# Building the stacked rank-16 factors on chip from eight raw copies, with VectorE and GpSimd in place of SBUF-to-SBUF transfers

## The reference, cut to what matters

```python
z1 = einsum('bfi,bir->bfr', x, u) / 512
z  = einsum('bfr,bor->bfo', z1, u) / 16
y  = einsum('bfi,oi->bfo', x, W) + fc_bias + z + cond
out = x + gelu(y)            # exact gelu, all in fp32
```

## Time and profile before

| | us |
|---|---|
| median of 3 runs | 387.24 (386.15 to 387.47) |
| the profiled execution's own time | 387.57 |
| its span, first to last instruction | 385.8 |
| TensorE busy | 376.9 (98% of the span) |
| VectorE busy | 296.7 (77%) |
| ScalarE busy | 204.6 (53%) |
| GpSimd busy | 0.7 |
| mean granted TensorE clock | 0.995 of full speed |
| DMA queue of SyncE | 27088 packets, 84.41 MB, 71.8% of the 16 engines' span |

### The profile page before, as it was taken

The page is one execution under the profiler, slowest core; times in us unless marked ns, Lnnn a source line. Parts: engine busy times, 40 slices in busy tenths (PEclk is TensorE's granted clock), DMA queues, the critical chain, the costliest instruction groups (busy, mean ns, idle before and its releaser), DMA issues.

```text
span 385.8 us, 7835 instructions
## 1 busy us (share of the span) xinstructions
PE 376.9 (98%) x3065; PEld 313.8 (81%) x3065; DVE 296.7 (77%) x188; ACT 204.6 (53%) x214; POOL 0.7 (0%) x5
## 2 busy tenths in 40 slices
PE   8998899999999999999999999999999999999995
PEld 3676788888888888888888888888888888888884
DVE  2579967788877878888777897778888787788832
ACT  3467364545566445566545556654465664455531
POOL 0000000000000000000000000000000000000000
PEclk9999899999999999999999999999999999999999
DMA  7879789887777877777787777687767779774222
GB/s 193 229 152 304 220 268 270 265 263 233 213 231 225 261 221 248 211 218 234 239 244 231 244 212 221 213 266 220 256 230 206 230 218 270 216 255 131 110 109 110
DMA packets 27756, 85.75 MB, mean 222 GB/s; under 512 B 6832, under 2 KB 6960, under 8 KB 23776
## 3 DMA queue, kind: packets, MB, share of 16 engines
q1 hardware_dynamic: 27088, 84.41, 71.8%
q10 hardware_dynamic: 656, 1.18, 1.0%
HBM read 35.75 MB, written 33.55 MB: 180 GB/s over the span
## 4 chain that ended last, share of the span: by engine, by line
PE 89%; SPq 5%; DMA 2%; ACTq 1%; ACT 1%; DVE 1%; issue 0%
PE y L420 82%; SPq L178 5%; PE update L489 3%; DMA f_stack<-f_parts 2%; ACTq L274 1%; PE y L404 1%; PE y L412 1%; PE y L408 1%; ACT L279 0%; SPq L164 0%; SPq L192 0%; ACT result L270 0%; DVE result L356 0%; DVE x_low L313 0%; DVE f_parts L313 0%
## 5 line engine op out<-in xcount | busy, mean ns | idle before, releaser
L420 PE MATMUL y<-x_low,w_high 64*128 64x512 f32 x928 | 184.5, 388 | 0.0
L420 PE MATMUL y<-x_high,w_high 64*128 64x512 f32 x928 | 184.5, 388 | 0.0
L270 ACT ACTIVATE result<-y,bias 128x512 f32<-128x512 f32 x128 | 81.4, 685 | 156.9 <-PE y L420 148.6
L420 PE MATMUL y<-x_high,w_low 64*128 64x512 f32 x928 | 125.2, 387 | 0.0
L356 DVE TENSOR_TENSOR result<-result,x_in 128x1024 f32<-128x1024 f32 (+1 forms) x65 | 78.3, 1205 | 56.5 <-ACT result L270 56.5
L420 PEld LDWEIGHTS y<-x_high,w_low 64*128 64x128 f32 x928 | 90.5, 185 | 15.3
L420 PEld LDWEIGHTS y<-x_low,w_high 64*128 64x128 f32 x928 | 90.5, 185 | 15.3
L420 PEld LDWEIGHTS y<-x_high,w_high 64*128 64x128 f32 x928 | 90.3, 185 | 15.3
L317 DVE SCALAR_TENSOR_TENSOR full_w<-update,base_w 128x2048 f32<-128x2048 f32 (+1 forms) x38 | 74.3, 1954 | 23.6 <-PE update L489 16.9
L313 DVE TENSOR_TENSOR x_low<-x_in,x_high 128x2048 fp32r<-128x2048 f32 (+1 forms) x38 | 74.0, 1947 | 5.6 <-ACT x_high L256 5.6
L313 DVE TENSOR_TENSOR w_low<-full_w,w_high 128x2048 fp32r<-128x2048 f32 (+1 forms) x38 | 74.0, 1948 | 0.4
(11 more groups left out here) (15 smaller groups left out, 29.7 us busy)
## 6 DMA issues: line engine op xcount, KB each, us to landing
out_t<-result SPq DMA_DIRECT2D x63, 512.0 KB, 3.1
x_in<-x_t SPq DMA_DIRECT2D x31, 1024.0 KB, 6.5
f_stack<-f_parts SPq DMA_DIRECT2D x186, 64.0 KB, 4.1
f_stack<-f_parts SPq DMA_DIRECT2D x124, 32.0 KB, 3.8
x_in<-x_t ACTq DMA_DIRECT2D x4, 256.0 KB, 9.3
base_w<-w_t SPq DMA_DIRECT2D x4, 256.0 KB, 8.2
f_parts<-factors SPq DMA_DIRECT2D x1, 896.0 KB, 6.8
out_t<-result SPq DMA_DIRECT2D x2, 256.0 KB, 2.5
```

What stands on the lines that cost most here:

```text
L270: nc.scalar.activation(result[j % SLOTS][:, m, :], y[m][:, :], ACT.Gelu, bias=bias[:, bass.ds(b * CHUNKS + m, 1)]).then_inc(gelu_ready, 1)
L420: return nc.tensor.matmul(y[m][:, :], w[rows, c, m * P:(m + 1) * P], x[rows, c, :], start=first, stop=last)
```

## The change

- The factors lie raw in DRAM, one [16, 512] matrix a batch. One DMA a batch reads it eight times over and fills the 128 rows of `f_raw` (four buffers). SyncE's 310 stack transfers are gone.
- Per batch ScalarE rounds all 128 rows (`high_factors`, L243), VectorE makes the weight side of the stack in one instruction, raw - high on the rows that are to hold the low part and raw elsewhere (`stack_factors`, L342), and GpSimd makes the moving side in two: `f_masked` = high * mask (L443) and raw + `f_masked` (L446). The mask is 0 or -1 for each row; GpSimd numbers the rows and VectorE turns the numbers into masks, once, at the start. The high blocks now hold the raw value, which TensorE takes in its place.
- TensorE's update waits for both sides. In the first two batches, the update of batch 1 stands ahead of piece 3 (before: ahead of piece 2) and waits for `full_w` chunk by chunk; the four first updates all stand ahead of piece 0, and `f_first` has 128 rows, of which 16 hold factors and the others zeros (two memsets on VectorE, the rest from DRAM).
- First loads: the weights lie chunk by chunk in DRAM; ScalarE's queue no longer loads factors between its first x chunks; SyncE issues the factors of batch 1 between the second and third weight chunk, and factors and x of batches 2 and 3 straight behind, with no wait.

Core of the diff:

```diff
-    STACK_DMAS = 5 * TILES
+    COPIES = P // RANK
...
         @block.sync
-            def stack_factors(t, j):
...
-                for copy in range(TILES):
...
-                        sp.dma_start(f_stack[slot][row + g * RANK:row + (g + 1) * RANK, sides, :].bitcast(fp32),
-                                     pair).then_inc(stacked[slot], 16)
-            sp.dma_start(f_first[:, :], factors[0:RANK, 0, :]).then_inc(f_first_loaded, 16)
+            def load_factors(t, j):
+                sp.dma_start(f_raw[j][:, :],
+                             factors[bass.ds(UNROLL * t + j, 1)].to_broadcast([COPIES, RANK, FEATURES])
+                             ).then_inc(f_loaded[j], 16)
+            sp.dma_start(f_first[0:FIRST_ROWS, :], first_factors).then_inc(f_first_loaded, 16)
             for c in range(CHUNKS):
-                sp.dma_start(base_w[:, c, :], w_t[:, c, :]).then_inc(w_loaded[c], 16)
+                sp.dma_start(base_w[:, c, :], w_t[c]).then_inc(w_loaded[c], 16)
+                if c == 1:
+                    load_factors(0, 1)
             load_x(0, 1)
...
-            sp.wait_ge(f_low_ready, 1)
-            stack_factors(0, 1)
-            stack_factors(0, 2)
-            sp.dma_start(f_parts[:, 1:GROUPS, 2, :], factors[:, 1:GROUPS, :]).then_inc(f_loaded[1], 16)
-            for j in range(2, X_SLOTS):
-                load_x(0, j)
+            load_factors(0, 2)
+            load_x(0, 2)
+            load_factors(0, 3)
+            load_x(0, 3)
...
         @block.scalar
+            def high_factors(t, j):
+                b = UNROLL * t + j
+                act.wait_ge(f_loaded[j], 16 * (t + 1) if j else 16 * t)
...
+                nc.scalar.activation(f_high[j % SLOTS][:, :], f_raw[j][:, :], ACT.Copy).then_inc(f_high_ready, 1)
...
                 elif not is_last(t, j):
                     split_x(tn, jn)
                     split_w(tn, jn)
+                    if not piecewise(t, j) and has_stack(t, j):
+                        high_factors(*stacked_in(t, j))
                 for m in range(CHUNKS if is_whole(t, j) else TILES):
                     gelu(t, j, m)
                 if piecewise(tn, jn):
                     for c in range(CHUNKS // 2, CHUNKS):
                         high_pieces(b + 1, c)
-                if j == 0 and not last_group:
-                    split_factors(t + 1)
+                if piecewise(t, j):
+                    high_factors(*stacked_in(t, j))
...
         @block.vector
+                nc.vector.scalar_tensor_tensor(f_stack[slot][:, 0, :], f_high[slot][:, :].bitcast(fp32),
+                                               low_rows[:, 0:1], f_raw[j][:, :], ALU.mult,
+                                               ALU.add).then_inc(weights_stacked, 1)
...
+            nc.vector.memset(f_first[FIRST_ROWS:2 * FIRST_ROWS, :], 0.0).then_inc(f_first_zeroed, 1)
+            nc.vector.memset(f_first[2 * FIRST_ROWS:P, :], 0.0).then_inc(f_first_zeroed, 1)
...
+                if has_stack(t, j):
+                    stack_factors(*stacked_in(t, j))
                 if piecewise(t, j):
                     finish_previous(t, j)
...
         @block.gpsimd
+                nc.gpsimd.tensor_scalar(f_masked[:, :], f_high[slot][:, :].bitcast(fp32), low_rows[:, 1:2], None,
+                                        ALU.mult).then_inc(factors_masked, 1)
+                pool.wait_ge(factors_masked, b)
+                nc.gpsimd.tensor_tensor(f_stack[slot][:, 1, :], f_raw[j][:, :], f_masked[:, :],
+                                        ALU.add).then_inc(moving_stacked, 1)
+            for b in range(1, BATCHES):
+                stack_factors(*divmod(b, UNROLL))
...
         @block.tensor
-            for c in range(CHUNKS - 1):
+            for c in range(CHUNKS):
                 first_update(c)
             for c in range(CHUNKS):
-                if c == 1:
-                    first_update(CHUNKS - 1)
-                if c == CHUNKS // 2:
+                if c == CHUNKS - 1:
                     rank_update(0, 1)
                 piece(0, c)
```

More of the change, by code:

```diff
@@ L39, in cond_residual_kernel @@
     GROUPS = BATCHES // UNROLL
-    RANK = factors.shape[0] // UNROLL
+    RANK = factors.shape[1]
+    FIRST_ROWS = first_factors.shape[0]
+    COPIES = P // RANK
     UPDATE_SCALE = 1.0 / (FEATURES * RANK)
@@ L72, in cond_residual_kernel @@
         result = [sb(f"result{s}", [P, CHUNKS, ROWS], fp32) for s in range(SLOTS)]
-        f_first = sb("f_first", [RANK, FEATURES], fp32)
-        f_parts = sb("f_parts", [UNROLL * RANK, GROUPS, 3, FEATURES], fp32)
+        f_first = sb("f_first", [P, FEATURES], fp32)
+        f_raw = [sb(f"f_raw{s}", [P, FEATURES], fp32) for s in range(UNROLL)]
+        f_high = [sb(f"f_high{s}", [P, FEATURES], fp32r) for s in range(SLOTS)]
+        f_masked = sb("f_masked", [P, FEATURES], fp32)
+        rows = sb("rows", [P, 1], int32)
+        row_bit = sb("row_bit", [P, 2], int32)
+        low_rows = sb("low_rows", [P, 2], fp32)
         f_stack = [sb(f"f_stack{s}", [P, 2, FEATURES], fp32r) for s in range(SLOTS)]
@@ L157, in previous_batch, with stacked_in, has_stack @@
             return (t, j - 1) if j else (t - 1, UNROLL - 1)
+        def stacked_in(t, j):
+            return t + (j + 2) // UNROLL, (j + 2) % UNROLL
+        def has_stack(t, j):
+            return not (isinstance(t, int) and t == GROUPS - 1 and j >= UNROLL - 2)
         block = ctx.enter_context(nc.Block())
@@ L199, in step @@
                 last_group = isinstance(t, int) and t == GROUPS - 1
-                if not (last_group and j >= UNROLL - 3):
-                    t3, j3 = t + (j + 3) // UNROLL, (j + 3) % UNROLL
-                    sp.wait_ge(update_ready, made(b + 1))
-                    stack_factors(t3, j3)
                 parts = [slice(0, HALF), slice(HALF, CHUNKS)]
@@ L361, in finish_previous @@
                     add_x(*previous_batch(t, j), slice(HALF, CHUNKS))
-                if j == 1 and not (isinstance(t, int) and t == GROUPS - 1):
-                    low_factors(t + 1)
             def step(t, j):
```

96 lines of the change are left out of this document (61 added, 35 removed).

## The result

The changed kernel takes **399.25 us** (median of 4 runs, 397.85 to 400.0), the kernel before 387.24. The ratio is 1.0335, with a 95% interval of 1.0296 to 1.0375: 12.0 us slower. The direction of the prediction was right, its size was not: 389.0 was forecast, and 399.25 lies outside 386.2 to 392.6. The profiled execution took 399.69 us, with a span of 397.9 and a mean granted clock of 0.985.

A forecast was written before the change was run, and what follows sets the result against it. TensorE, busy in 98% of the span, was taken as the bound. Loop 0 and batch 3's update +1.75 us gave 387.24 + 1.75 = 389.0 us, range 386.2 to 392.6.

The forecast's parts named there:

- Cost in the loop: 0: Later batches: the added ScalarE, VectorE and GpSimd work fits, GpSimd's pair having 5.5 us of room; cost 0.
- The last rival: Loop: GpSimd's pair overruns its 5.5 us, for instance waiting out `w_low`; 415 us or more; chance 0.05.
- upper bound of 2.6: GpSimd's pair: 0.52 us for every operand read or written, two in the first instruction, three in the second.
- I take 2.1: GpSimd's two stack instructions with the hand-over between them: 2.1 us, between bounds of 1.04 and 2.6.
- Steps 1 and 2: Start: piece 0 at 10.0 us at the high clock; update of batch 1 at 18.2 instead of 18.83.
- Steps 3 and 4: Start: batch 1's last `w_high` ends at 27.9; rounding 0.63 and GpSimd 2.1 put batch 2's update at 30.6 us.
- Step 5: Start: from batch 2's update to the end of batch 1's gelus 7.33 us as before, ending at 37.9.
- Step 6: Start: rounding 0.63, GpSimd 2.1 and a wait of 0.69 put batch 3's update at 41.4, +1.75 us.
- the third rival: Start: GpSimd and VectorE hold each other up; update of batch 3 at 45.7, 393.3 us; chance 0.15.
- The slow clock behind it I leave as it is: Behind batch 3's update: the slow clock costs batch 2's products 1.65 us, before and after the change.
- Taking them away gives nothing back: Loop: the transfers that fill the stacks cost nothing in these batches, so removing them gains nothing.

The follow-up runs named there:

- run 1: Changed kernel with the factors' rounding moved ahead of `w_high` on ScalarE from batch 2 on: 394.01 us.
- run 5: Changed kernel with GpSimd's addition done twice, the first into a tile that nobody reads: 459.32 us (one run).
- run 6: run 4 with GpSimd doing the same two instructions on tiles of its own, nobody waiting for them: 395.68 us.
- run 8: Changed kernel with the four first updates multiplying only the 16 rows of `f_first` that hold factors: 403.97 us.
- run 4: Changed kernel with VectorE making both sides of the stack and GpSimd none: 387.69 us.
- run 2: Changed kernel with batch 3's factors rounded between `x_high` and `w_high` of batch 2, not behind batch 1's gelus: 395.9 us.
- run 7: run 6 with GpSimd's pair replaced by one memset of 128x3072 that reads nothing from on-chip memory: 388.33 us (one run).

## Why the prediction was wrong in size

- **The loop, "Cost in the loop: 0": wrong, +6.8 us.** This is the larger half of the loss. The step compared a pair price of 2.1 with 5.5 us of room. The room was about right: 5.7 us by the rows above, 11.33 less the 5.64 from the update to the end of the rounding. The price was wrong: the pair takes 5.6 us there (191.14 to 196.73), which with 0.3 us for the hand-overs on both sides of it overruns the room by 0.23. The next batch's chain starts at the late update, so this is lost anew in every batch: 11.56 us against 11.33. Runs 1 and 5 show it from both sides. The last rival named the mechanism, waiting out `w_low`, and had 0.05 of the chance; but it priced the overrun at a full 1 us a batch (415 or more). Most of its working was at hand: 2.3 us of `w_low` on top of a pair near its upper bound of 2.6 is already 4.9, with 0.6 left of the room.
- **GpSimd's price, "I take 2.1": wrong.** Alone it is 2.91 (run 6), outside even my upper bound of 2.6. That bound gave the masking 1.04 and the addition 1.56; they take 1.57 and 1.26, and 0.08 lies between them. In company the pair takes 3.5 to 5.6 in the changed kernel, and up to 6.1 in run 1.
- **Steps 1 and 2: right in mechanism.** The pace of the products rose during the first updates, even earlier than forecast: piece 0 at 8.79 (forecast 10.0), update of batch 1 at 17.27 (18.2). Run 8 shows that the zero rows do this. The prediction calls the two paces the low and the high clock; the granted clock reads 1.00 in both there (see the last section).
- **Steps 3 and 4: the right time by two errors that cancel.** The update of batch 2 came at 30.76 (forecast 30.6). The last `w_high` of batch 1 ended at 26.58, 1.3 us before the forecast, and the pair took 3.46, 1.4 us more than forecast.
- **Step 5, "7.33 us": wrong, +1.4.** It is 8.7 (30.76 to 39.46). I took the old row pair as it was, and didn't ask what the wait before the update of batch 2 does. The granted clock fell to 0.50 behind it, the gelus of batch 1 waited 0.83 us for TensorE, and they took 2.74 instead of 2.40.
- **Step 6, "0.63 + 2.1 + 0.69": wrong, +1.8.** From the end of the gelus to the update it is 5.23 us, because the masking, beside VectorE's stack instruction and two additions of x, took 3.17 instead of 1.57. This is the third rival (mutual waits, 45.7; 44.69 measured), which had 0.15. Steps 5 and 6 with the 0.16 of step 4 make the 3.3 us between the forecast of 41.4 and 44.69.
- **"The slow clock behind it I leave as it is": right** in the two profiled executions, 13.33 against 13.26 us.
- **"Taking them away gives nothing back": right.** The DMA queue's share fell from 71.8% to 54.5%, and run 4, with the whole change but GpSimd's part, is 0.5% slower than the kernel before, not faster.

How the loss splits between loop and start rests on the times of the updates and on runs 1, 2 and 4. That the fall of the clock behind batch 2's update lengthened step 5 is read from the rows and wasn't tried alone.

## What to carry to other kernels

Room in a schedule has to be compared with what an instruction takes in the company it will have there, not alone: GpSimd's masking, which reads on-chip memory, took 1.57 us alone and 4.2 beside VectorE's wide two-input instructions. Before calling an idle engine free, follow its new work round the loop: if it hangs on something that the last update released and the next update waits for it, its whole latency is in a closed chain, and starting it earlier can be worth as much as making it shorter (run 1: a longer pair and a shorter period). And a start that is mended shows the next wait: a late load and a place in VectorE's order each gave back most of a gain here, until the whole sequence had been moved.

## What the runs showed of the hardware that I had not expected

- A one-input multiply with a mask on GpSimd, 128x512 in fp32, takes 1.57 us alone, more than the two-input addition of the same size (1.26), and 4.1 us in company.
- VectorE pays too: its addition of x went from 1.22 to 2.30 us where GpSimd's addition had started 0.17 us earlier (run 6). A memset of 2.67 us, which reads nothing, made no instruction of VectorE longer (run 7).
- Padding a 16-row product with 112 rows of zeros brought the update of batch 1 some 4 us earlier (run 8). The granted clock of the windows doesn't show this: it reads 1.00 in both kernels there, while the spacing of the products differs by nearly two. At the very start the pace has to be read from the products. The windows of run 8 (first row) and of the changed kernel (second), each in its piece 0:

```profile
11.00:12.00 1.00, 1.00 (x3) 0.81 (x3) 0.51 (x2) 0.79 (x2) 0.00 (x0) 1.00 1.06 424
```

```profile
9.00:10.00 1.00, 1.00 (x6) 0.82 (x5) 0.54 (x2) 0.16 (x1) 0.00 (x0) 1.00 1.07 201
```

- TensorE waited 2.18 us before the update of batch 2 in the changed kernel, and behind that the granted clock was 0.50, from 31.7 to about 34.3. In run 2 it fell behind a wait of 1.77 us. The kernel before falls behind its 2.24 us in the profiled execution; its two groups of times, told apart by the mean granted clock, suggest that it doesn't in every execution. Only the one was traced, so this isn't shown.
